# State-space steps taken in pairs across head groups

## What is computed

```python
proj = x @ W_in.T + b_in                 # gate 2048, h 2048, B 128, C 128, dt 32
hBC = silu(causal_conv4(hBC))            # 4 taps along the tokens
h = h * dt; A_cum = cumsum(A * dt)
Y_diag = ((C @ B.T) * exp(segsum(A * dt))) @ h       # inside a chunk
Y_off  = (C @ state) * exp(A_cum)                    # from the chunks before
state  = exp(A_cum_last) * state + (B * decay).T @ h
y = Y_diag + Y_off + D * h
g = y * silu(gate); g = g * rsqrt(mean(g * g)) * norm_w
out = g @ W_out.T + b_out
```

## Time and profile before

| | us |
|---|---|
| median of 3 runs | 2265.36 |
| lowest and highest | 2261.38, 2267.99 |
| the profiled execution | 2262.73 |
| its span, first to last instruction | 2261.0 |
| state-space stage, about | 151 to 1380 |

### The profile page before, as it was taken

One profiled execution on the slowest core, in us unless ns is written; L12 is line 12 of the kernel. 1 busy time (PEld: TensorE's weight loads), 2 busy tenths in 40 slices (PEclk: granted clock), 3 DMA queues, 4 the chain that ended last, 5 costly groups with the idle time before them and its releaser, 6 DMA issues. The chain is left out here.

```text
span 2261.0 us, 43811 instructions
## 1 busy us (share of the span) xinstructions
PE 2124.2 (94%) x13681; PEld 1685.8 (75%) x13681; DVE 1575.2 (70%) x3408; ACT 1266.4 (56%) x2754; POOL 1414.6 (63%) x1248
## 2 busy tenths in 40 slices
PE   4878999999999999999999998999989989999997
PEld 2446777777777777777777776877744779999997
DVE  5778888888888888888888884676766853333332
ACT  2456777777777777777777772222235653333332
POOL 1325777777777777777777775777764624444443
PEclk9999999999999999999999999999999999999999
DMA  9854445545554455454545544886473065232221
GB/s 321 333 135 119 135 144 147 152 137 146 145 156 135 144 148 151 139 146 143 150 140 145 141 133 140 254 268 217 151 261 118 1 222 137 48 50 47 46 46 24
DMA packets 193458, 328.83 MB, mean 145 GB/s; under 512 B 49043, under 2 KB 135188, under 8 KB 192980
## 3 DMA queue, kind: packets, MB, share of 16 engines
q1 hardware_dynamic: 135972, 227.40, 34.1%
q0 software_dynamic: 26640, 53.38, 9.1%
q10 hardware_dynamic: 30624, 45.25, 6.5%
HBM read 240.19 MB, written 86.53 MB: 145 GB/s over the span
## 5 line engine op out<-in xcount | busy, mean ns | idle before, releaser
L1014 DVE SCALAR_TENSOR_TENSOR m_cv<-m_hp,conv,m_cv 128x256 f32<-128x256 f32 x864 | 416.7, 482 | 112.2 <-ACT m_cv L913 91.0
L840 POOL TENSOR_TENSOR m_er<-m_er,m_cT 128x1024 f32<-128x1024 f32 x128 | 302.3, 2362 | 43.7 <-DVE m_ar L1021 43.7
L951 ACT ACTIVATE m_ar<-m_ar,m_ta 128x128 f32<-128x128 f32 x1024 | 318.9, 391 | 0.8
L1102 PE MATMUL m_hp<-xnT,wpj 128*128 128x259 f32 x1152 | 304.7, 387 | 7.8 <-PEq L145 4.5
L1110 PE MATMUL m_gp<-xnT,wpj 128*128 128x256 f32 x1024 | 268.2, 384 | 11.2 <-ACT m_gT L931 11.2
L1538 PE MATMUL e_u<-e_xgT,xnT 128*128 128x128 f32 x2272 | 266.9, 276 | 1.0 <-ACT xnT L1476 1.0
L1102 PEld LDWEIGHTS m_hp<-xnT,wpj 128*128 128x128 f32 x1152 | 214.1, 192 | 68.7 <-issue 28.3
L1538 PEld LDWEIGHTS e_u<-e_xgT,xnT 128*128 128x128 f32 x2272 | 260.9, 193 | 1.3 <-ACT xnT L1476 1.2
L847 POOL TENSOR_TENSOR m_hdd<-m_hdt,m_tb 128x512 f32<-128x512 f32 x128 | 131.0, 1043 | 193.6 <-DVE m_hdt L1029 193.6
L931 ACT ACTIVATE m_gT<-m_gp,bias 128x256 f32<-128x256 f32 x256 | 121.4, 474 | 230.6 <-PE m_gp L1110 178.5
L1161 PE MATMUL m_out<-wo,m_gT 128*128 128x256 f32 x1024 | 242.9, 380 | 0.0
(11 more groups left out here) (338 smaller groups left out, 4260.8 us busy)
## 6 DMA issues: line engine op xcount, KB each, us to landing
m_ar<-acum_rows_dram SPq DMA_DIRECT2D x512, 128.0 KB
m_er<-eacum_rows_dram SPq DMA_DIRECT2D x128, 512.0 KB, 4.3
rows_by_slot<-blank_rows ACTq DMA_DIRECT2D x1, 18576.0 KB, 81.0
e_xg<-rows_by_slot ACTq DMA_DIRECT2D x131, 129.0 KB
m_xrow<-xn_rows SPq DMA_DIRECT2D x32, 512.0 KB, 5.1
arena<-y_rows SPq DMA_DIRECT2D x16, 1024.0 KB, 7.2
arena<-in_w SPq DMA_DIRECT2D x5, 1024.0 KB
wpj<-in_w_proj SPq DMA_DIRECT2D x1, 4352.0 KB, 23.6
```

Of the source, the lines that this page charges most:

```text
L840: g.tensor_tensor(er[:, t], er[:, t], middle(cT[:, t * P:(t + 1) * P], HQ), ALU.mult).then_inc(scaled.sem, 1)
L951: ins = a(row, row, ACT.Exp, bias=ta[:, t, q * HQ + h:q * HQ + h + 1])
L1014: v_.scalar_tensor_tensor(o, hp[n % 2][:, j:j + BLK], conv[:, c, j:j + 1], o, ALU.mult, ALU.add).then_inc(tapped.sem, 1)
L1102: ins = mm(hp[n % 2][:, 0:PW], w_proj[:, kd, col:col + P], xpad[:, kd, ds(i * BLK, PW)], start=kd == 0, stop=kd == KD - 1)
```

## The change

Steps are paired otherwise. Before, a slot computes t = 0 and t = 1 of one head group, the second after the first. Now slot n computes step `a` = (group of slot n-2, t = 1) and step `b` = (group of slot n-1, t = 0). They belong to different head groups, so neither needs the other's state. TensorE issues `from_state` and `inside` of a and then of b in one stretch, updates a, and updates b at the slot's end. The output product of a follows late projection 2; that of b (`last`, one slot later) is cut into two halves of two channels, behind the third and the fourth gate projection. There is one more slot to drain (`DEPTH = 3`). Since a may belong to the block before, the tables `ta`, `tb`, `gm` and `btok` get a third row. VectorE finishes a step before it adds the state, and at q = 0 copies C last of the four. GpSimd's queue and SyncE's loads follow the same pairing.

The core of the diff:

```diff
-DEPTH = 2
+DEPTH = 3
 
 
 def slots(body):
@@ -705,7 +705,37 @@
         def at(lag):
             i, q = divmod(n - lag, NQ)
             return (i, q) if 0 <= i < NB else None
-        body(at(0), at(1), at(2))
+        body(n, at(0), at(1))
+
+
+def older(m):
+
+    return divmod(m - 1, NQ) + (1,) if 0 < m <= NB * NQ else None
+
+
+def newer(m):
+
+    return divmod(m, NQ) + (0,) if 0 <= m < NB * NQ else None
+
+
+def pair(m):
+
+    return [s for s in (older(m), newer(m)) if s]
+
+
+def kept(i, t):
+
+    return 1 + i % 2 if t else 0
+
+
+def both(i):
+
+    return slice(0, 2 + i % 2, 1 + i % 2)
+
+
+def last_of(step):
+
+    return step is not None and step[1] == NQ - 1 and step[2] == TB - 1
...
+                def decay_rows(i, q, t):
+                    s = q * TB + t
+                    off.wait(sp, i, s - 1)
+                    src = rows_e[ds(i * TB + t, 1), q * HQ * P:(q + 1) * HQ * P]
+                    sp.dma_start(er[:, t].rearrange("p h l -> p (h l)"),
+                                 src.rearrange("a n -> (a n)").partition_broadcast(P)).then_inc(s_er[t], 16)
...
+                    a, b, last = older(n - 1), newer(n - 1), newer(n - 2)
+                    if b:
+                        mixed.wait(pool, b[0], b[1] * TB + 1)
+                        scale(*b)
+                    if last:
+                        add_squares(*last)
+                    if a:
+                        weigh(*a)
+                    if b:
+                        weigh(*b)
+                    if a:
+                        age(*a)
+                    if b:
+                        age(*b)
+                    if last and last[1] == NQ - 1:
+                        fold_squares(last[0], 0)
...
+                        scale(*u, 1)
+                    if a:
+                        add_squares(*a)
+                        if last_of(a):
+                            fold_squares(a[0], 1)
...
+                    for step, chunk in ((older(n), 0), (newer(n), 1)):
+                        lead = chunk + 1
+                        if step:
+                            exps(*step, range(0, lead))
+                        if late[chunk] is not None:
+                            first_tap(w[0], late[chunk])
+                        if step:
+                            exps(*step, range(lead, HQ))
+                    step = older(n - 1)
...
+                    if step:
+                        square(*step)
...
+                    if a:
+                        mix(*a)
+                    if b:
+                        mix(*b)
...
-                    if u:
-                        grow(*u, 0)
-                        finish(*u, 0)
+                    if a:
+                        finish(*a)
+                        grow(*a)
                     if w:
                         taps(w[0], late[1])
-                    if u:
-                        finish(*u, 1)
-                        grow(*u, 1)
+                    if b:
+                        finish(*b)
+                        grow(*b)
...
                     for c in range(CQ):
@@ -1181,28 +1231,27 @@
                                 turn(u[0], 1)
                         if soon[c] is not None:
                             project(w[0], soon[c])
+                        if c >= 2 and last:
+                            project_out(*last, range(c * 2 - 4, c * 2 - 2))
                         if u:
-                            if u[1] == 1 and c == 0:
+                            if u[1] == 2 and c == 0:
                                 ss_kept.wait(pe, u[0], 0)
                             turn(u[0], 2 + u[1] * CQ + c)
                     if w:
                         project(w[0], late[0])
-                    if u:
-                        from_state(*u, 0)
-                        inside(*u, 0)
-                        update(*u, 0)
+                    for step in pair(n - 1):
+                        from_state(*step)
+                        inside(*step)
+                    if a:
+                        update(*a)
                     if w:
...
-                    if v:
-                        project_out(*v, 1)
-                    if u:
-                        from_state(*u, 1)
-                        inside(*u, 1)
-                        update(*u, 1)
-                    if v and v[1] == NQ - 1:
-                        add_up(v[0])
-                    if u:
-                        project_out(*u, 0)
+                    if a:
+                        project_out(*a)
+                    if b:
+                        update(*b)
+                    if last_of(older(n - 2)):
+                        add_up(older(n - 2)[0])
```

More of the change, by code:

```diff
@@ L967, in body @@
                             first_tap(w[0], soon[c])
[L968 to L976 removed]
+                        if c == 1 and last:
+                            square(*last)
+                    for step, chunk in ((older(n), 0), (newer(n), 1)):
[7 more added lines that the diff above has]
+                    step = older(n - 1)
+                    if last_of(step):
+                        i = step[0]
                         outd.wait(act, i, STEPS)
@@ L1171, in add_up, with body @@
                     ins.then_inc(ss_done.sem, 1)
-                def body(w, u, v):
-                    soon, late = fresh(w[1]) if w else ([None] * 4, [])
+                def body(n, w, u):
+                    soon, late = fresh(w[1]) if w else ([None] * 4, [None] * 2)
+                    a, b, last = older(n - 1), newer(n - 1), newer(n - 2)
                     if u and u[1] == 0:
```

120 lines of the change are left out of this document (46 added, 74 removed).

## The result

The changed kernel takes 2341.1 us (median of 4 runs, 2338.3 to 2344.4) where the kernel before, on the same chip, takes 2264.1 (4 runs, 2261.4 to 2268.0): 1.034 times as long, 95% interval 1.032 to 1.036. The forecast was 2325, between 2285 and 2345. The profiled execution has a span of 2339.0 us against 2261.0, 78 us more. Its page, against the earlier trace rows: TensorE's work is the same to the tenth of a microsecond and its share is 91% instead of 94%. VectorE has 38 us more, without a new instruction.

A forecast was written before the change was run, and what follows sets the result against it. TensorE's queue was taken as the bound before; after the change, late VectorE and ScalarE chains. Profiled time 2262.7, +57 for 15 blocks, 0 for the first block, +5 for the end: 2325 us, range 2285 to 2345.

The forecast's parts named there:

- the case given 0.50: VectorE's and ScalarE's chains both late, one gating held by a GpSimd addition: 2325 us, chance 0.50.
- the rival with the mixes held: In slot 0's tail VectorE's mixes also wait for GpSimd's addition: +0.55 us in 15 blocks, 2333 us, chance 0.20.
- The tail after h, and the cycle: TensorE's work from h to slot end falls from 7.28 to 3.55 us; from T to the next h 9.82.
- h: Start of a slot's second late projection, the one in mid-tail, from which the forecast counts its times.
- Slot 1 to 2: From slot 1's tail to slot 2's: T at h+8.5 plus 9.82 us, 18.32 us.
- T: Time at which the next slot's second head transpose goes out on TensorE; h+8.5 in the plain case.
- VectorE's chain: VectorE's work from taps to the next slot's first keep ends last, narrowly, releasing the second transpose at h+8.5.
- stretch 2 to 3: From slot 2's tail to slot 3's: gating held by GpSimd's addition, T at h+9.25, 20.81 us.
- ScalarE's chain: ScalarE's SiLU begins at h+5.21; with the gate eviction behind it, T not before about h+8.1.
- Slot 3 to 0: From slot 3's tail to slot 0's: first product waits for SiLU, second transpose 4.81 us later plus 0.2: 20.72 us.
- Slot 0 to 1: From slot 0's tail to slot 1's: block output copy makes SiLU about 1.07 us later, T h+9.15, 18.97 us.
- The ends: At the kernel's end the extra half step runs alone, less what the shorter last slot saves: +5 us, between 2 and 8.

The follow-up runs named there:

- the two fillers: 0.87 us of matmuls with unused result added to TensorE's queue in each slot: on the kernel before 2316.7 us, on the changed kernel 2343.6 us.

## Why the prediction was right, and where its sizes were off

The direction and the mechanism were right. The time, 2341.1, lies 16 us above the 2325 of the sum and 4 below the end of the range, and the case given 0.50 was not the one that came: it was the rival with the mixes held, and the low clock came on top, which the sum had at nothing.

*TensorE's queue is the bound.* Shown by the two fillers: +53 us of 54 before; after, nothing of 0.87 in three stretches and all of it from 1 to 2.

*The tail after h, and the cycle.* The forecast 3.55 from h to the slot's end measured 3.46, and TensorE's saving turned into waits. At full clock a block has 72.38 us of work against 73.11: 0.73 less, where the half-width products in one stretch were to save 4 times 0.14, or 0.56. It idles 6.8 us of 79.18 there, as the "7 or so" had it. Over all 59 slots the saving can't be seen (1077.18 against 1077.33), because the low clock gives it back.

*Slot 1 to 2.* 18.32 forecast, 18.06 measured: T is h+8.37 (765.52 to 773.89), released by ScalarE's SiLU and not by the keep, and from there to the next h it is 9.69 instead of 9.82.

*VectorE's chain.* T = h+9.25 in stretch 2 to 3 came out as h+9.17, with the held gating (1.54) that the step named. Cutting the addition took 0.82 away, which shows the cause. The stretch is still 0.25 longer than forecast, since between T and h the next projection starts 0.3 late (714.02, where 712.86+0.87 would be 713.73). I had not counted that. `project` waits for the taps of the projection two before it, and these stand behind the late keep and end at 713.96:

```profile
712.45 1.51 DVE L1059 SCALAR_TENSOR_TENSOR m_cv<-m_hp,conv,m_cv 128x256 f32<-128x256 f32 x3
...
714.02 1.14 PE L1150 MATMUL m_hp<-xnT,wpj 128*128 128x259 f32 x4
```

The run with the later mix makes the same wait 1.23 long.

*ScalarE's chain* was called narrowly second. It is more often the one that releases TensorE (in the 59 slots 49 waits and 70 us, against 30 and 20 us for the keep), and the run with the later mix shows that it is right behind the keep. "VectorE's chain ends last" was too strong; both had to be named as the bound, and from 1 to 2 ScalarE's copy of the sums, which ties it to TensorE, had no place in the sum.

*Slot 3 to 0.* 20.72 forecast, 20.84 in eight blocks; in seven it takes 0.97 (five) or 1.5 more (two). There the transposes wait 2.37 us, and behind them TensorE runs in part on the lower of its two levels, 1.2 GHz (granted clock 0.61 over 4.35 us):

```profile
730.48:734.83 4.35, 4.35 (x17) 3.52 (x17) 3.04 (x7) 1.55 (x4) 1.65 (x2) 0.61 0.73 187
```

The step "from there the second transpose took 4.81 us" took the clock of the kernel before for granted. Term: +0.45 a block, 7 us, at nothing in the sum. Where the wait was 1.85 (square later) or 1.51 (filler) this stretch had no such block.

*Slot 0 to 1.* This is the rival "mixes held as well", given 0.20, and it is the case: 3.62 instead of 2.35, the rival's T = h+9.7 came out as h+9.49 (746.28 to 755.77). By the rule of the Trainium skill (SBUF — State Buffer, section "SBUF: two separate sides") that was due; the first run with the mixes beside such an addition agrees. It cost 0.35 on the path.

*The ends.* I took +5 and it was +10.2. The extra half step itself is about as costed. Half of the 10.2 stands ahead of it: "less what the shorter last slot saves" did not come, since from its first gate projection to its pair the last slot takes 11.55 us (1425.43 to 1436.98) where the kernel before takes 6.26 (1358.62 to 1364.88), with waits of 1.51 and 1.66 before its transposes, 1.7 of output product and a granted clock of 0.85. The other half is behind it. The last sum of squares is serial there: output product, its copy, the square, GpSimd's addition and two folds, 4.49 us of wait where the kernel before waits 1.67. I had no term for that. The kernel after, then the one before:

```profile
1450.70 1.99 PE L1209 MATMUL m_out<-wo,m_gT 128*128 128x256 f32 x8 [0.42 <-DVE m_gT L1098]
1457.18 1.02 PE L1219 MATMUL m_tr<-ones,m_sqf 128*128 128x1 f32 x4 [4.49 <-POOL m_sqf L907]
```
```profile
1379.05 0.61 PE L1170 MATMUL m_tr<-ones,m_sqf 128*128 128x1 f32 x4 [1.67 <-POOL m_sqf L872]
```

The first block gave 2.2 back, inside its range of 4. Decay rows at 0 held: they land a little later (median 4.6 us, longest 6.5, against the earlier trace rows) and TensorE waits for them nowhere that counts.

Together: +69.0 for the slots (forecast 56), -2.2 for the first block, +10.2 for the end (5), +1.0 elsewhere, 78.0.

## What to carry to other kernels

Where TensorE's queue is the bound, what stands in it between a projection and the first instruction that needs its result is cover for the other engines' chain, even if it is itself useful work: before moving it, work out by how much that chain has room, and move no more than that and no more than the waits it fills. Moving an operation of GpSimd or ScalarE out of the way helps only if the place where it lands is free: look at which VectorE operation, or which eviction, it will stand beside or ahead of. Extra work put into one queue tells which engine is the bound only if it is read stretch by stretch: a total can hide a stretch in which all of it shows.

## What the runs showed that I had not expected

- A copy of only 128x64 elements on VectorE (0.35 us) is held as well: begun while a scatter runs and 0.35 ahead of GpSimd's addition (712.88 and 713.23), it takes 1.70 and ends 0.07 after the addition. In the changed kernel it begins beside a scatter alone (709.75) and takes 0.35. A gating begun 0.28 behind an addition ends 0.55 after it. State additions and output products, which read PSUM, kept 0.68 and 1.11 beside the same operations (751.15 beside the addition of 751.36).
- Behind the same wait of 2.37 us, TensorE's clock fell in 7 of 15 blocks and not in 8; what decides it these runs don't tell.
- In the run with the later square it fell in 6 of 15 stretches 0 to 1 instead, behind waits of 1.07 and 0.61 us with a pair of transposes between them.
